# A reordered start and end for a two-layer graph attention kernel, with two column loads on another queue

## What is computed

```
# layer A
q, k, v = x @ Wq.T + bq, x @ Wk.T + bk, x @ Wv.T + bv        # 8 heads of 32
pros = softmax(where(adj == 0, MASK_VAL, q k^T))
z = v;  repeat 4 times: z = 0.9 * pros @ z + 0.1 * v
x = norm(x + z) * gamma + beta
# layer B
nx = norm(x) * ln1_g + ln1_b
q, k, v = nx @ wq + bq, nx @ wk + bk, nx @ wv + bv
attn = softmax(q k^T / sqrt(32) + where(adj > 0, 0.1 * adj * adj, -inf))
x1 = x + (attn @ v) @ wo + bo
n2 = norm(x1) * ln2_g + ln2_b
out = x1 + gelu(n2 @ w1 + b1) @ w2 + b2
```

## Time and profile before

| | us |
|---|---|
| median of 3 runs | 2275.35 (2273.99 to 2276.94) |
| the profiled execution | 2275.21 |
| its span, first to last instruction | 2273.3 |
| TensorE busy | 2242.9 (99%) |
| ScalarE busy | 1925.4 (85%) |
| VectorE busy | 1738.3 (76%) |
| GpSimd busy | 1522.4 (67%) |
| TensorE's granted clock, mean | 0.996 |

### The profile page before, as it was taken

The page is one execution under the profiler, slowest core; times in us unless marked ns, Lnnn a source line. Parts: engine busy times, 40 slices in busy tenths (PEclk is TensorE's granted clock), DMA queues, the critical chain, the costliest instruction groups (busy, mean ns, idle before and its releaser), DMA issues.

```text
span 2273.3 us, 78265 instructions
## 1 busy us (share of the span) xinstructions
PE 2242.9 (99%) x29492; PEld 2135.4 (94%) x29492; DVE 1738.3 (76%) x6993; ACT 1925.4 (85%) x6478; POOL 1522.4 (67%) x1613
## 2 busy tenths in 40 slices
...
GB/s 128 19 37 32 35 39 21 39 35 24 39 26 35 39 23 37 39 21 39 39 21 39 28 32 39 25 34 39 21 39 39 21 39 31 29 39 25 32 14 20
DMA packets 95781, 76.88 MB, mean 34 GB/s; under 512 B 9648, under 2 KB 95152, under 8 KB 95408
## 3 DMA queue, kind: packets, MB, share of 16 engines
q1 hardware_dynamic: 94176, 71.73, 10.4%
...
...
## 4 chain that ended last, share of the span: by engine, by line
PE 93%; DVE 3%; ACT 2%; issue 1%; POOL 0%; SPq 0%; DMA 0%; ACTq 0%; DVEq 0%; POOLq 0%
PE ring_ps L393 40%; PE ring_ps L531 15%; PE ring_ps L475 13%; PE ring_ps L467 10%; PE score_ps L458 6%; PE ring_ps L495 5%; PE ring_ps L418 3%; ACT probs L596 1%; DVE probs L720 0%; PE ring_ps L404 0%; DVE hT_low L806 0%; DVE nx L800 0%; DMA g_col<-in_L_gnn_ln_g_dram 0%; POOL probs L878 0%; ACT hT_high L637 0%
## 5 line engine op out<-in xcount | busy, mean ns | idle before, releaser
L596 ACT ACTIVATE probs<-probs,negmax 128x128 f32<-128x128 f32 x2048 | 796.6, 397 | 10.8 <-DVE negmax L720 4.7
L878 POOL TENSOR_TENSOR probs<-probs,rinv 128x512 f32<-128x512 f32 x512 | 535.9, 1068 | 112.5 <-DVE rinv L734 112.3
L596 ACT ACTIVATION_READ_ACCUMULATOR probs<-probs,negmax 128x1 f32 x2048 | 401.2, 196 | 0.0
L617 ACT ACTIVATE zT<-ring_ps 128x512 f32<-128x512 f32 x256 | 157.5, 615 | 176.8 <-PE ring_ps L475 176.4
L393 PE MATMUL ring_ps<-inT_C_high,w_high 128*128 128x256 f32 x1024 | 300.1, 293 | 0.0
L531 PE MATMUL ring_ps<-w_high,hT_high 128*128 128x256 f32 x1024 | 296.3, 289 | 1.4 <-DVE probsT_B L745 0.9
L467 PE MATMUL ring_ps<-ident,probs 128*128 128x128 f32 x2048 | 293.3, 276 | 1.6 <-ACT hT_high L637 0.7
L531 PE MATMUL ring_ps<-w_low,hT_high 128*128 128x256 f32 x1024 | 285.9, 279 | 0.0
L531 PE MATMUL ring_ps<-w_high,hT_low 128*128 128x256 f32 x1024 | 285.9, 279 | 0.0
L393 PE MATMUL ring_ps<-inT_C_high,w_low 128*128 128x256 f32 x1024 | 283.9, 277 | 0.0
L393 PE MATMUL ring_ps<-inT_C_low,w_high 128*128 128x256 f32 x1024 | 283.8, 277 | 0.0
...
## 6 DMA issues: line engine op xcount, KB each, us to landing
...
out_dram<-x SPq DMA_DIRECT2D x128, 128.0 KB, 2.0
...
```

The lines of the kernel that those rows point to most:

```text
L596: e = act.activation(probs[:, u, h, :], probs[:, u, h, :], ACT.Exp, bias=negmax[:, u, h:h + 1], scale=-1.0, accum_out=sums[:, u, h:h + 1])
L617: act.activation(zT[k][:, :, :, :], ring(name, g).rearrange("p (b c n) -> p b c n", b=GB, c=C), ACT.Copy).then_inc(s_out[name], 1)
L878: pool.tensor_tensor(probs[:, u, hs, :], probs[:, u, hs, :], rinv[:, u, hs].unsqueeze(2).to_broadcast([P, HR, P]), ALU.mult).then_inc(s_pr ...
```

## The change

The two columns of the third norm (ln2_b and ln2_g, `h2_col` and `g2_col`) are no longer issued by SyncE behind w1 in `load_up`, but by ScalarE in the list of small loads at its start. They still count on the semaphore "up", and nobody's wait is changed. HEAD and TAIL are written anew: each holds the same steps as before, in another order. ORDER, the functions of the steps and all sizes stay.

```diff
             def load_up(name, g):
                 weight(w1_raw, w1, "up")
-                column(h2_col, ln2_b, "up")
-                column(g2_col, ln2_g, "up")
...
         @block.scalar
         def _(act):
-            for t, w, signal in ((colA["q"], bq, "colA"), (colA["k"], bk, "colA"), (h1_col, ln1_b, "B"), (g1_col, ln1_g, "B")):
+            for t, w, signal in ((colA["q"], bq, "colA"), (colA["k"], bk, "colA"), (h1_col, ln1_b, "B"), (g1_col, ln1_g, "B"),
+                                 (h2_col, ln2_b, "up"), (g2_col, ln2_g, "up")):
...
 HEAD = """
-laA.0 xs.0 Wk.0 Wq.0 LB.0 eb.0 laB.0 mA00.0 qA.0 mA01.0 msA.0 mA10.0 kA.0 Lc.0 Wu1.0 mA11.0 eA00.0 vA.0 lt.0 xs.1 sA.0
-Wf.0 rA1.0 msB.0 eA10.0 wA1.0 vA.1 wA0.0 Lu.0 eA11.0 rA0.0 msA.1 eA01.0 Wu0.0 qA.1 Wv.0 kA.1 pA10.0 pA11.0 pA00.0
...
+laB.0 Wu1.0 qA.0 xs.0 kA.0 vA.0 msA.0 mA00.0 Wu0.0 sA.0 mA01.0 Wo.0 mA10.0 eA00.0 eA01.0 Lu.0 mA11.0 eA10.0 rA0.0
+eA11.0 xs.1 eb.0 Wf.0 msA.1 kA.1 rA1.0 wA0.0 vA.1 qA.1 wA1.0 pA00.0 pA01.0 pA10.0 pA11.0 sA.1 xv.0 Wq.0 msB.0 mA00.1
+mA01.1 laA.0 z0.0 eA00.1 xs.2 h0.0 mA10.1 eA01.1 eA10.1 rA0.1 z1.0 wA0.1 msA.2 wA1.1 mA11.1 eb.1 eA11.1 xv.1 lt.0 kA.2
+h1.0 qA.2 Lo.0 rA1.1 LB.0 z2.0 lt.1 pA00.1 pA01.1 Wd3.0 pA10.1 Wd0.0 h2.0 pA11.1 Wd2.0 sA.2 i0.0 z3.0 xs.3 z0.1 mA00.2
+eA10.2 mA01.2 mA10.2 Lc.0 lx.0 g.0 h3.0 eA00.2 laA.1 y0.0 h0.1 n0.0 Wd1.0 Lr.0 vA.2 i1.0 z1.1 h1.1 eA01.2 msA.3 mA11.2
+rA0.2 qA.3 z2.1 y1.0 Wv.0 kA.3 eA11.2 lt.2 h2.1 n1.0 wA0.2 vA.3 Wk.0 rA1.2 z3.1 tB.0 h3.1 y0.1 pA00.2 pA01.2 Ld.0 kB.0
...
 TAIL = """
...
+eB01.1 wB1.2 o.2 y2.2 mB01.1 mB10.1 n2.2 eB10.1 mB11.1 b2.3 msB.1 rB0.1 vB.1 d0.3 tC.2 rB1.1 d1.3 eB11.1 i2.2 pB00.1
+u0.2 wB0.1 b1.1 pB10.1 wB1.1 pB01.1 c0.2 u1.2 i2.1 pB11.1 u2.2 c1.2 pv.1 c2.2 c3.2 b2.2 u3.2 o.1 y2.1 n2.1 d0.2 tC.1
+d1.2 b2.1 c0.1 c1.1 u0.1 u1.1 u2.1 c2.1 st.1 u3.1 c3.1 d0.1 d1.1
```

More of the change, by code:

```diff
@@ L56 @@
[L56 to L75, removed]
```

71 lines of the change are left out of this document (42 added, 29 removed).

## The result

| | us, median | runs |
|---|---|---|
| before | 2275.83 (2273.99 to 2277.08) | 7 |
| the changed kernel | 2266.67 (2265.40 to 2268.45) | 7 |

The ratio is 0.996, with a 95% interval from 0.995 to 0.997: 9.2 us faster. Medians are over all runs of a kernel, of which a few in the experiments took far longer (2469 us and more), and the ratios leave those out. The profiled execution of the changed kernel has a span of 2265.1 us, 8.2 us less than before.

What follows compares the result with a forecast made beforehand. TensorE bounds the steady turns; the start is bound by loads, then fold, then probabilities. Gains of 5.7 + 1.8 + 1.0 = 8.5 us off 2275.2 gave 2266.7 us, range 2258.5 to 2273.5.

Steps and rivals of the forecast that it cites:

- Loads: At the start, at 308 GB/s, w1 is there at 12.1 us and the second layer's weights at 16.0; fold starts at 16.0.
- rival of late loads: At the start, loads come at 134 GB/s until 15 us, the fold starts at 18.5: 2271.9 us; chance 0.16.
- The columns' queue: At the start, columns issued by ScalarE are there by about 10 us, before w1; the queue itself was taken as nothing.
- The fold's clock: In the fold, the clock falls at 18.7 us again; the fold ends at 25.6 instead of 31.2.
- the rival that it stays: In the fold, the clock doesn't fall and the fold ends at 22.2 us: 2262.4 us in all; chance 0.17.
- The first hop: After the second pair's projections, the first hop begins 5.7 us earlier, at 33.9 us.
- The hops: Among the first hops, moved projections cover 2.4 us of waits, moved splits take back 0.6: gain 1.8, bounds 0 and 6.5.
- The last turns: After 1950 us, waits totalling 3.6 us may go or be replaced: gain 1.0 us; the 2.2 us wait stays.
- The rival of a long new wait with a fall of the clock: In the last turns, each such wait costs 9.9 us: one 2276.6 us, chance 0.10; two 2286.5, chance 0.04.

Runs made afterwards that it cites:

- experiment 4: The changed kernel with the third norm's two columns issued by SyncE again, behind w1: 2268.11 us, ratio 0.9968 to the kernel before.
- experiment 1: The kernel before with only the third norm's two columns moved to ScalarE, old HEAD and TAIL: 2274.37 us, ratio 0.9994.
- experiment 6: The kernel before with the fold's one-column products made 64 columns wide: 2275.57 us, ratio 1.0001.
- experiment 5: The changed kernel with the fold's one-column products made 64 columns wide: 2262.68 us, again 2261.69; with 16 columns 2268.28.
- the second profile: The changed kernel run again unchanged: 2267.31 us, ratio 0.9961 to the kernel before.
- the wide fold: The changed kernel with the fold's products 64 columns wide: 2262.68 us, and 2261.69 us in the run of its second profile.

## Why the prediction was right

The time, 2266.7 us, was met, and so was the mechanism in its main parts: an earlier fold, a clock that falls inside it, an earlier first hop. That the number came out to 0.1 us is luck, since the errors in the terms largely cancelled, and two profiles of this one kernel differ by 0.2 us at the 4000th matmul. Term by term:

**Loads.** At 308 GB/s the prediction had w1's split at 12.1 and the fold at 16.0; measured 11.96 and 15.81. The rate in 10 to 15 us was 344 GB/s instead of 134, as the column elements had moved behind. The rival of late loads didn't occur. But the 12.1 was hit by luck: w1 was there at 11.3, 0.8 earlier than I had it, and what the split waited for was the column.

**The columns' queue.** I had the columns there by about 10 us, ahead of w1. That was wrong: the last took 8.6 us instead of the 5.4 of my row, which is of a column issued at 1.76, and came at 11.9, behind w1. I took nothing for two more issues on ScalarE, because they filled the 1.02 us in which it waited. They cost 0.5: ScalarE's first split started at 6.13 instead of 5.63 without any wait before it, and TensorE's first matmul 0.49 us later. (Over all profiles that matmul came at 7.50 to 8.06 with seven issues on ScalarE and at 7.14 to 7.22 with five.) The cover was measured up to the first activation, but a table load stands between the issues and that; it moved from 3.32 to 4.83 and ends now after the weights have come. The earlier columns give some 0.8 us at the fold (experiment 4), but only in the new order, where w1 is early (experiment 1).

**The fold's clock.** The forecast, that it falls during the fold though TensorE has no pause before it, was right, and the rival that it stays was wrong as the kernel stands. The Trainium skill (TensorE: Matmul & The Clock Gate, Part 1) has the clock released by activity and a busy engine warm; the trace here disagrees for the fold, where TensorE was busy from 7.63 us on and the clock fell at 20.3. My reason for the fall was weaker than it looked: it was that one-column products had run for 12.3 us at 1.2 GHz before, and experiment 6 shows that in that place wide ones do so too. Those 12.3 us did not tell what narrow products do to a clock that is up; experiment 5 does. I had it fall at 18.7 and rise 1.7 us into the projections; it fell at 20.3 and rose 3.6 us into them. Fold's end: 25.6 predicted, 23.5 measured (the start of the next matmul). End of the projections: 30.5 and 29.6. Experiment 5 shows what that fall still costs: 3.6 to 4.0 us in the profiles, 4.0 to 5.6 in the times.

**The first hop.** 33.9 predicted, 32.5 measured, in a profile with the short slow stretch. Others with this HEAD, or one changed only behind the fold, had 33.0 to 36.1, so the 5.7 us that I took are inside what was seen (3.5 to 7.1).

**The hops.** 1.8 predicted, 1.85 measured (8.94 less 7.09). The term was right by errors that cancelled: the projections did take away waits of 2.1 us (L493 from 4.7 to 2.6; 3.8 in the second profile), Wq, which I had not seen on VectorE ahead of h0.0, brought the new 1.63 us wait, and a slow stretch of 3.4 us behind that, which no term had, cost up to 1.7. The size that I gave back belonged to another split.

**The last turns.** Predicted a gain of 1.0, measured a loss of 0.7. This step failed. It rested on no row: I took a share of 3.6 us of waits as if a new order had to be better. New waits of 1.31, 1.35 and 0.69 came in place of 0.92, 0.51 and 0.55. All waits there together went from 6.3 to 7.8 us, more than the 0.7 that was lost; where the new order gave the rest back isn't shown. The rival of a long new wait with a fall of the clock did not occur, though the clock's fall at the 2.2 us wait, in both kernels, is itself not certain: in the second profile of the wide fold and in that of experiment 4 that wait brought no fall.

Sum as measured: 7.1 (with -0.5 in it) + 1.85 - 0.7 = 8.2 us of span, against 5.7 + 1.8 + 1.0 = 8.5.
